# A transformer layer with a routed MLP: attention heads on 32 rows with a constant shift, and no break between the two attentions

## What is computed

```python
x = L0_attn_x                                        # (1, 2048, 128)
# attention 1: 16 heads of 8, rotary, causal
Q, K, V = heads(x @ wq.T), heads(x @ wk.T), heads(x @ wv.T)
Q, K = rope(Q), rope(K)
A = softmax(where(causal, Q @ K.T / sqrt(8), -inf))
x = layernorm(x + merge(A @ V) @ wo.T)
y0 = x
# attention 2: 16 heads of 8, every row sees every row
q, k, v = split((layernorm(x) * ln1_w + ln1_b) @ w_qkv)
x = x + merge(softmax(q @ k.T / sqrt(8)) @ v) @ w_proj
# MLP: each row goes to one of 8 experts (128 -> 512 -> 128, gelu)
h = layernorm(x) * ln2_w + ln2_b
e = argmax(h @ gate_w + gate_b)
x = x + gelu(h @ w1[e]) @ w2[e]
out = layernorm(y0 + x)
```

## Time and profile before

| | us |
|---|---|
| median of 3 runs (lowest, highest) | 1054.88 (1051.29, 1055.4) |
| time of the profiled execution | 1064.6 |
| its span | 1062.8 |
| PE busy | 905.1 (85%) |
| ACT busy | 800.5 (75%) |
| DVE busy | 361.5 (34%) |
| POOL busy | 232.3 (22%) |

### The profile page before, as it was taken

The page is one execution under the profiler, slowest core; times in us unless marked ns, Lnnn a source line. Parts: engine busy times, 40 slices in busy tenths (PEclk is TensorE's granted clock), DMA queues, the critical chain, the costliest instruction groups (busy, mean ns, idle before and its releaser), DMA issues.

```text
span 1062.8 us, 24412 instructions
## 1 busy us (share of the span) xinstructions
PE 905.1 (85%) x9808; PEld 400.9 (38%) x9822; DVE 361.5 (34%) x1022; ACT 800.5 (75%) x908; POOL 232.3 (22%) x361
## 2 busy tenths in 40 slices
PE   4586999999998954999999999999999999995261
PEld 2243444334443422343344444433444434443031
DVE  6551453421432043410014333143332433334662
ACT  7165788789898923999999998968889889982240
POOL 6341212111110111000003233222232132331243
PEclk9767999899999976999999999968999879996575
DMA  8795012010035126800020000300000010000101
GB/s 246 143 135 120 2 42 42 1 41 3 2 73 68 31 30 106 174 6 2 3 41 27 2 2 3 66 11 26 2 3 17 12 36 2 1 12 16 35 1 35
DMA packets 30258, 43.03 MB, mean 40 GB/s; under 512 B 3904, under 2 KB 14656, under 8 KB 30144
## 3 DMA queue, kind: packets, MB, share of 16 engines
q1 hardware_dynamic: 28576, 37.75, 18.0%
q0 software_dynamic: 1536, 3.67, 1.2%
q10 hardware_dynamic: 32, 0.03, 0.0%
HBM read 28.73 MB, written 12.45 MB: 39 GB/s over the span
## 4 chain that ended last, share of the span: by engine, by line
PE 70%; DVE 9%; DMA 7%; ACT 6%; issue 4%; SPq 2%; POOL 1%; POOLq 0%; ACTq 0%; DVEq 0%
PE ps L437 66%; DMA k_scratch<-parts 4%; ACT probs L862 4%; PE ps L442 3%; PE ps L694 2%; ACT key_rows L899 1%; DMA query_rows<-neg_shift_final 1%; SPq L329 1%; ACT squares_blockdiag L876 1%; SPq L321 1%; DVE ln_stats L1079 1%; DVE ln_newton L1072 1%; DVE ln_newton L1073 1%; DVE ln_newton L1074 1%; DVE squares_blockdiag L1371 1%
## 5 line engine op out<-in xcount | busy, mean ns | idle before, releaser
L862 ACT ACTIVATE probs<-ps 128x1024 f32<-128x1024 f32 (+3 forms) x832 | 746.1, 1002 | 128.8 <-PE ps L437 126.0
L437 PE MATMUL ps<-probs,values 128*9 128x256 f32 (+1 forms) x6528 | 446.6, 388 | 1.9 <-DVE q_rotated L1227 0.8
L437 PE MATMUL ps<-query_rows,key_rows 33*128 33x512 f32 (+3 forms) x1664 | 336.9, 469 | 30.6 <-DMA query_rows<-neg_shift_final 13.3
L437 PEld LDWEIGHTS ps<-probs,values 128*9 128x9 f32 x6528 | 145.9, 91 | 225.4 <-issue 127.0
L437 PEld LDWEIGHTS ps<-query_rows,key_rows 33*128 33x128 f32 x1664 | 142.7, 193 | 215.6 <-ACT probs L862 116.3
L972 POOL TENSOR_SCALAR_AFFINE_SELECT probs<-probs 128x256 f32<-128x256 f32 x128 | 53.5, 418 | 268.9 <-ACT probs L862 266.8
L1005 POOL COPY expert_stage<-early_late 128x512 f32 x72 | 46.0, 677 | 161.9 <-PE ps L437 161.9
L1227 DVE COPY q_rotated<-ps 128x512 f32<-128x512 f32 x32 | 22.1, 690 | 161.6 <-PE ps L437 161.5
L986 POOL DMA_INDIRECT z_sorted<-z_rows,row_shift x16 | 15.8, 990 | 237.5 <-issue 168.6
L1001 POOL COPY expert_stage<-parts 128x512 f32 x72 | 47.9, 709 | 54.0 <-PE ps L437 48.6
L937 ACT ACTIVATE expert_stage<-parts 128x512 f32 x24 | 15.1, 630 | 48.8 <-DVE row_shift L1366 27.5
(11 more groups left out here) (168 smaller groups left out, 625.7 us busy)
## 6 DMA issues: line engine op xcount, KB each, us to landing
query_rows<-q_scratch SPq DMA_DIRECT2D x64, 128.0 KB
key_rows<-k_scratch SPq DMA_DIRECT2D x20, 256.0 KB, 7.7
q_scratch<-parts SPq DMA_DIRECT2D x8, 512.0 KB, 3.4
k_scratch<-parts SPq DMA_DIRECT2D x8, 512.0 KB, 3.7
key_rows<-k_scratch SPq DMA_DIRECT2D x16, 192.0 KB, 6.5
parts<-in_w SPq DMA_DIRECT2D x1, 2048.0 KB, 18.1
early_late<-in_w SPq DMA_DIRECT2D x8, 256.0 KB, 5.8
early_late<-z_sorted SPq DMA_DIRECT2D x4, 384.0 KB, 3.0
```

Of the source, the lines that this page charges most:

```text
L437: return nc.tensor.matmul(out, l, r, start=start, stop=stop, skip_group_check=True)
L862: nc.scalar.activation(Pr[:, i % 2, 2 * p:2 * p + 2, lo:BLK], score_banks(t, p)[:, :, lo:BLK], ACT.Exp, scale=SCALE).then_inc(s["exp"], 1)
```

## The change

- A head takes 32 rows. The shift is one constant per attention (0 and 58), the bias of the exp. The row of ones, the shift rows, their DMAs, `shift`, `shift_turn`, `take_shift`, `settle` and the fills of `key_rows` are gone. Four heads of a group lie at partitions 0, 32, 64 and 96, so pair 1 has places of its own.
- One check per attention (`bound`, `check`, `count_ok`, `take_ok`): the product of the largest norms has to lie under shift + 72, and a lower bound of each row's maximum (diagonal score, or best of the first 32 keys) over shift - 66. It runs at steps 1 and 9 of block (1,0), and 38 and 42 of (2,0). If it fails, `general` computes whole blocks in another way: loops over groups, tiles and heads with register-counted waits on PE, ACT and DVE. It stands in the last group of each block, behind a branch on each of the three engines; the flag is read once per attention.
- Scratch holds each part twice (`(2, NP, NP, DK, H, S)`), so rows of a block, keys or queries, come back in four transfers of 32 rows. Parts have a slot for each block.
- SP: small weights first, without a wait; the input rows (`x_rows`), the mask and the clearing of `z_sorted` come after the key rows of attention 1. Key rows for attention 2 go group by group into its early steps, those of the last block later.
- Attention 2 follows attention 1 in one list of runs. Block (2,0) has the order (g0, 12 steps), (g1, 12), (g0, last 4), (g1, last 4), g2, g3, with half sums kept in `sums_so_far`, and carries the side work of block 3 of attention 1. V of attention 2 has a tensor of its own.
- Row minima over 32 keys (4 matmuls per block for 8). The projections of a block start with the keys.

```diff
-        KA = sb("key_rows", [P, PAIRS * S], F32R)
-        QA = sb("query_rows", [P, 2 * PAIRS * BLK], F32R)
+        KA = sb("key_rows", [P, G * S], F32R)
+        QA = sb("query_rows", [P, 2 * G * BLK], F32R)
...
-        k_scratch = nc.dram_tensor("k_scratch", (2, NP, DK, H, S), F32, kind="Internal").ap()
+        k_scratch = nc.dram_tensor("k_scratch", (2, NP, NP, DK, H, S), F32, kind="Internal").ap()
...
+            def rows_in(rows, scratch, a, g0, g1, t0, t1, done):
+
+                src = scratch[a - 1].rearrange("i j d (g f) t -> f (i j d) g t", f=HG)
+                for f in range(HG):
+                    sp.dma_start(rows[f * ROWS:(f + 1) * ROWS], src[f, :, g0:g1, t0:t1]).then_inc(done, 16)
...
+            keys_out(1, 0)
+            queries_out(1, 0)
+            first_key_rows(0)
+            query_rows(1, 0)
+            keys_out(1, 1)
+            queries_out(1, 1)
+            first_key_rows(1)
+            query_rows(1, 1)
+            keys_out(1, 2)
+            first_key_rows(2)
+            keys_out(1, 3)
+            first_key_rows(3)
+            queries_out(1, 2)
+            queries_out(1, 3)
+
             sp.dma_start(xn[:, :, :], x_d.rearrange("(t p) d -> p t d", p=P)).then_inc(ld_x, 16)
+            sp.dma_start(cmask, cmask_d).then_inc(ld_c, 16)
...
+            for g, r in enumerate(runs_in(1, NB - 1)):
+                sp.wait_ge(S_set, 2 * (r["t0"] + S // P))
+                rows_in(kaf[:, g:g + 1, 0:OLD * P], k_scratch, 2, g, g + 1, 0, OLD * P, k_early[g])
+            query_rows(2, 1)
+            keys_out(2, NB - 1)
+            sp.wait_ge(k_out[NB - 1], 64)
+            rows_in(kaf[:, :, OLD * P:S], k_scratch, 2, 0, G, OLD * P, S, k_late)
...
-            def scores(s, slot, g, kt_at, t, lo, p):
-
-                if 2 * t + p:
-                    pe.wait_ge(s["exp"], 2 * t + p)
-                for hh in range(2):
-                    rows = slice(hh * HALF, hh * HALF + KR)
-                    pair = g * HG // 2 + p
-                    last = mm(score_banks(t, p)[:, hh, lo:BLK], KAv[rows, pair, kt_at:kt_at + P], QAv[rows, slot, pair, lo:BLK])
-                last.then_inc(s["S"], 1)
+            def scores(step):
+
+                r, t = step["r"], step["t"]
+                for p in range(2):
+                    if 2 * t + p:
+                        pe.wait_ge(exp, 2 * t + p)
+                    for hh in range(2):
+                        rows = slice((2 * p + hh) * ROWS, (2 * p + hh + 1) * ROWS)
+                        last = mm(score_banks(t, p)[:, hh, step["lo"]:BLK],
+                                  KAv[rows, r["g"], step["kt"] * P:(step["kt"] + 1) * P],
+                                  QAv[rows, r["qb"] % 2, r["g"], step["lo"]:BLK])
+                    last.then_inc(S_set, 1)
...
-                for n in range(4):
+                for n in (2, 3, 0, 1):
...
             key_norms(1, 0)
             query_norms(1, 0)
-            settle(1)
-            general(1, 0, 0)
...
+                    nc.scalar.activation(Pr[:, t % 2, 2 * p:2 * p + 2, lo:BLK], score_banks(t, p)[:, :, lo:BLK],
+                                         ACT.Exp, bias=-SHIFT[r["a"]], scale=SCALE).then_inc(exp, 1)
...
+            def evac(r):
+
+                dve.wait_ge(pv, 2 * (LEAD + r["t0"] + r["k1"] - r["k0"]))
+                if r["opens"] and r["closes"]:
+                    ins = copy(accs[:, :], sums)
+                elif r["closes"]:
+                    ins = tt(accs[:, :], sums, half[:, r["g"], :], ALU.add)
+                else:
+                    ins = copy(half[:, r["g"], :], sums)
+                ins.then_inc(evac_done, 1)
...
-                if b >= 2:
-                    act.wait_ge(s["parts_out"][b % 2], 32 * (b // 2))
```

More of the change, by code:

```diff
@@ L96, with general_tiles @@
 OPS = len(IN_SHADE)
[L99 to L105, removed]
+def general_tiles(a, qb):
+    banks = qb + 1 if a == 1 else NB
+    return banks, sum(b + 1 if a == 1 else NB for b in range(qb))
 def build(nc, xT_d, x_d, wa_d, wo_d, wqkv_d, wproj_d, ln1w_d, ln1b_d, ln2w_d, ln2b_d, gw_d, gb_d,
@@ L400, in sorted_rows @@
+            for e in range(E):
+                sp.dma_start(W2v[:, e], w2_d[e].rearrange("(c p) n -> p c n", p=P)).then_inc(ld_m, 16)
             def sorted_rows(b):
@@ L606, in values @@
+            def values(step, p):
+                r, t, lo = step["r"], step["t"], step["lo"] // P
+                vals = Vv if r["a"] == 1 else V2v
+                pe.wait_ge(exp, 2 * t + p + 3)
                 if step["cut"] is not None:
-                    pe.wait_ge(s["dg"], step["cut"] + p)
-                if step["start"] and p == 0 and n:
-                    pe.wait_ge(s["evac"], n)
+                    pe.wait_ge(cut_done, step["cut"] + p)
+                if step["start"] and p == 0 and r["n"]:
+                    pe.wait_ge(evac_done, r["n"])
@@ L797, in side1, with run @@
-            def side1(qb):
-                if qb == 0:
-                    return side0(1)
-                b = qb - 1
-                at = SIDE1_AT[qb]
+            def run(r, side, freed, old):
+                mine = [run_step(r, n) for n in range(r["k1"] - r["k0"])]
+                keys_there(r)
+                for n, step in enumerate(mine):
+                    pos = r["at"] + n
+                    scores(step)
+                    if n == 0 and old:
+                        values(old[-2], 1)
+                        values(old[-1], 0)
+                    elif n == 1 and old:
+                        values(old[-1], 1)
+                    elif n == 2:
+                        values(mine[0], 0)
+                    if n >= 2:
+                        values(mine[n - 2], 1)
+                        values(mine[n - 1], 0)
+                    if n == TURN_STEP and old and old[-1]["r"]["closes"]:
+                        turn(old[-1]["r"], next((c[1:] for c in reversed(freed) if c[0] < pos), None))
+                    if n == TURN_STEP and r["last"]:
+                        general(r["a"], r["qb"], step["t"] + 1)
+                    for f in side.get(pos, ()):
+                        f()
+                return mine
@@ L874, in tanh, with attention @@
+            def attention(a, qb):
+                for r in runs_in(a, qb):
+                    for n in range(r["k1"] - r["k0"]):
+                        exps(run_step(r, n))
+                        if n == TURN_STEP and r["last"]:
+                            general(a, qb)
+                        if a == 2 and qb and r["at"] + n in TANH_AT:
+                            tanh(qb - 1, TANH_AT[r["at"] + n])
             def tanh(b, r):
@@ L1482, in _ @@
                 norms1(b)
-            attention(1)
-            b = NB - 1
+            dve.wait_ge(ld_e, 16 * 10)
+            dve.wait_ge(init, 3)
+            for a in (1, 2):
+                for qb in range(NB):
+                    attention(a, qb)
+            norm(2 * NB * G - 1)
+            settled(2, NB - 1)
+            post(2 * NB - 1)
             at_once = lambda step: None
-            rows_to_h(b, at_once)
-            split2(b, at_once)
-            settle(2)
-            attention(2)
             b = NB - 1
```

1065 lines of the change are left out of this document (458 added, 607 removed), and 7 rows, old and new, of tables (PREP_AT, SIDE1_AT).

## The result

The changed kernel takes 974.33 us in the median of four runs (974.13 to 978.01), the kernel before 1054.7 beside it (1051.29 to 1055.4). The ratio is 0.9252, 95% interval 0.9223 to 0.9282: 80.4 us less. The forecast was 938 with 905 to 992 around it. The time lies in the wide range, but 36 us over the forecast and outside the narrower range around it (918 to 955).

The account below looks back on a forecast made before the run. ScalarE was taken to bound (2,0), TensorE (2,1) to (2,3). Savings of 117.1 us from the profiled 1064.6 gave 947.5, less 9.7 for that execution's excess over the median: 938 us, range 905 to 992.

Parts of the forecast that it names:

- before the first exp: Prologue up to the first exponential: bound chain moved out, fewer waits, keys projected first; 14 us less.
- between the attentions: Almost idle stretch between attentions 1 and 2: its 38.6 us go, with 2 us added to block (2,0).
- The wait before (1,1): Idle before block (1,1), where TensorE waited for block 1's shift row: 9.1 us go.
- the small edits: Fewer row-minimum matmuls, counted within the score gain; ScalarE's branches and register loads cost 0, at most 3 us.
- Rival 4: TensorE, resting in ScalarE-bound steps, falls to 1.2 GHz: 1140 us if half of all steps ran so; chance 0.06.
- Scores on 32 rows: Score pairs overlap by 0.21 us: 32.4 us saved in (2,1) to (2,3); 4, 6, 8 in (1,1) to (1,3).
- the 3 us for the clock in (1,1): Block (1,1) ran at 0.93 of the clock after the wait before it: another 3 us saved.
- (1,2) and (1,3): Blocks 2 and 3 of attention 1: overlapping scores, at 0.125 us per step, save 6.0 and 8.0 us.
- the last subtraction: Whole kernel: 9.7 us taken off because the profiled execution lay that far over the median, giving 938 us.
- Rival 1: Score pairs in the attentions still stream in turn, so the overlap savings are lost: 986 us; chance 0.20.
- Rival 2: Input rows for (1,1) or last keys of attention 2 come late, costing 5 to 15 us: 950; chance 0.12.
- Rival 3: Attention gains more than 0.15 us a step; a third of the way to ScalarE's pace: 915 us; chance 0.09.

Follow-up runs that it names:

- e2: Changed kernel with the general path and its branches left out on TensorE, ScalarE and VectorE: 976.03 us, ratio 0.9194.
- e10: e9 with heads 2 and 3 reading the rows of heads 0 and 1, so score pairs can't overlap: 961.26 us, ratio 0.9059.
- e9: Changed kernel with experts' work a step earlier, other side work moved, and GpSimd's four indirect transfers one per step: 947.38 us, ratio 0.8942.
- e1: Changed kernel with heads 2 and 3 reading the rows of heads 0 and 1, so score pairs can't overlap: 985.12 us, ratio 0.9291.
- b1: Kernel before, with the turn of the expert rows, the gate and the ranks one step later: 1050.4 us, ratio 0.9906.
- e8: Changed kernel with each transfer bringing in key or query rows split in two of 16 rows: 980.59 us, ratio 0.9267.
- e6: Changed kernel with GpSimd's four indirect transfers to the sorted list made plain ones, the sort left out: 960.39 us, ratio 0.9093.
- e4: Changed kernel with GpSimd waiting for step 17's exps before the four indirect transfers, in three of four times: 976.85 us, ratio 0.9196.
- after_again: Changed kernel run once more without an edit, against the kernel before: 972.99 us, ratio 0.922.

## Why the prediction was right and where it was wrong

**Right: the start and the two waits.** Steps "before the first exp" (14, measured 15.6) and "between the attentions" (38.6, measured 38.6, with 0.6 and not 2 us added to (2,0)) are 54.2 of the 90.4 us saved in the profile. They were read off the trace as stretches in which ScalarE has nothing to do, and what has no work on it can be priced by its length. These are comparisons of the two profiles; neither was undone in a run. "The wait before (1,1)" (9.1 with 4 for (1,0)) came to 8.8 together: 2.07 us of ScalarE's idle time stayed at the block's start, 1.1 of it TensorE waiting on nothing that the profile shows. e2 had it too (1.89 us), so it isn't a branch. (1,0) itself gave the rest, 1.7 us in place of 4.

**Right: the small edits.** ScalarE's branch at 0, at most 3 us: e2 finds nothing to gain. The general path didn't run. Rival 4, the clock, didn't come: it was 0.99 in (2,0), with TensorE's rests of 0.4 us a step. The Trainium skill ("TensorE: Matmul & The Clock Gate", "Part 1: The HAM clock gate") lets the clock follow how busy TensorE has been. The falls that the two kernels' traces show in (2,1) to (2,3) come with TensorE waits of 1.4 us and more, but the one fall in (2,0) of the changed kernel does not: the longest wait in the 8 us ahead of it is 0.41 us.

```profile
344.19:347.60 3.41, 3.41 (x36) 1.10 (x32) 0.00 (x0) 2.42 (x4) 0.00 (x0) 0.50 1.06 223
```

What made it fall isn't shown; as it is, short rests don't exclude a fall, but it was one of 3.4 us and not the half of all steps that rival 4 priced.

**Wrong: "Scores on 32 rows".** The size of one overlap was right: 0.21 predicted, 0.22 measured, and the value matmuls follow after 0.44 us. By the 3.07 of the Trainium skill ("TensorE: Matmul & The Clock Gate", "Part 3: Packing small matmuls") it would have been 0.15, an estimate from the page's figure; the trace shows the full stream saved at each place where no exp is awaited. The count of steps was wrong. I took 0.15 us in each of 192 steps, because ScalarE's busy share of 0.85 to 0.91 and TensorE's 0.97 made TensorE the bound. That mean mixes two steps in six in which ScalarE waits 0.56 us with four in which it doesn't wait at all, and it counts the two pauses per block as if they were steady load. e10 against e9 gives 10.8 us in these blocks and 12.4 in all; the prediction had 50.4 (32.4 and 18) from the same cause. Inside the changed kernel, e1, it was 5.6 there and 4 to 11 in all. The expected pace of 1.9 to 2.1 us a step became 2.11 to 2.16.

**Wrong: the 3 us for the clock in (1,1).** It was 0.93 of full speed in that block before and 0.92 after, so this term gave nothing. The overlap, for which the prediction had 4 us here, gave 0.1 (e10 against e9) to 0.5 (e1). (1,1) saved 2.0 us in place of 7.

**Right by luck: (1,2) and (1,3).** They saved 4.0 and 8.1 us where the prediction had 6 and 8 for the overlap. Without the overlap the two take 208.8 us together in e1 and 205.8 in e10, against 215.9 before: 7.1 to 10.1 of the 12.2 us came from something else. A part of it is a pause of the kernel before at step 39 of (1,3), amid the matmuls for the row minima, of which the change halves the number:

```profile
335.75 1.02 ACT L862 ACTIVATE probs<-ps 128x1024 f32<-128x1024 f32 x1 [3.12 <-PE ps L437]
```

The changed kernel has no pause over 1 us in this block, nor have e1 and e10. The prediction put these matmuls "inside the 0.15". That the halving removed the pause isn't shown.

**Right by luck: part of what the last blocks did give.** Of the 12.1 us saved in (2,1) to (2,3), the clock's long falls alone are worth more: b1 removes them with a single step of distance and saves 14.2 us there in its profile. In the changed kernel they are gone as well, and what came in return is the pause at step 17, 1.96 to 2.36 us in each block with a short fall of the clock at it. The prediction named neither. Why the changed kernel has no long fall behind its wait at step 10 of (2,2) stays open; e1 has none either, so the overlap isn't the reason.

**Wrong: the last subtraction.** The sum gave 947.5 us for the profiled execution, and I took 9.7 off because the profile of before lay that far over its median, which I put down to the falls in (2,2) and (2,3). By the prediction's own numbers these cost 11.8 and 7.2 us, 19.0 together, not 9.7. And the changed kernel doesn't have them: its profiled execution (974.19) is at its median (974.33). What the falls cost was thus already in the savings, and had not to be taken off again. Without this step the forecast is 947.5. Of the 36 us missed, 26.7 are the terms (20.3 of them in the three blocks, 5 in (1,1), 4.3 in (1,0)) and 9.7 this step.

**The rivals.** Rival 1 (986) was nearer than the forecast, for another reason than its own: the scores do get faster, but ScalarE waits for them in two steps of six only. Rival 2 (data late) didn't come: the input rows were issued at 68.6 us, landed 10.2 later and were first used at 89.9, some 11 us to spare. With twice the issues before them (e8) they were issued at 83.8, and VectorE waits 8.1 us for them. Rival 3's price has a slip: its span of 880 is a time of 882, and a third of the way there from 938 is 919, not 915.

## What to carry to other kernels

Before a saving on one engine is multiplied by the number of steps, look at the other engine's timeline over one period of the pattern and count the steps in which it waits: two in six here. A pause with a place (a step, a transfer, a bank) was worth more here than a faster instruction: moving side operations by one step and spacing four transfers gave some 30 us on top of the 80 (0.031 of the ratio). A pause also takes back a part of what is saved ahead of it (5.6 us in place of 10.8), so take the pauses first.

## What the runs showed of the hardware

Four indirect transfers that GpSimd issues 1.3 us apart, each 0.96 to 1.01 us long in (2,2), go with TensorE's signals reaching ScalarE and VectorE up to 3 us late. ScalarE goes on some 0.8 to 1.1 us after the last transfer. Plain transfers of the same rows from the same queue take 0.5 to 0.7 us each there and show none of it (e6), nor do indirect ones 1.8 to 2.2 us apart (e9). What holds the signals stays open: in (2,1) of e4 and in all three blocks of the kernel before (two of them at half clock then), four in a row passed without a pause of that size.

TensorE's clock fell for 27.3 and 17.1 us behind a wait of TensorE of 1.43 us in the kernel before. In `after_again` it fell for 3.4 us at a wait of the same 1.43 us in (2,2) and in (2,3), and in the changed kernel's first profile for 3.4 to 6.8 us at waits of 2.5 to 2.8 us. How long a wait is doesn't say how long the clock stays down.
